# A Mamba layer on one core: the B rows broadcast to SBUF by DMA, and a fifth pair of states turned by TensorE with its products made on POOL

## The reference, cut to what matters

```python
def step(h, inp):
    xt, dt_, bt, ct = inp
    dA = jnp.exp(dt_[..., None] * A)
    h = dA * h + dt_[..., None] * bt[:, None, :] * xt[..., None]
    y = jnp.einsum('bdn,bn->bd', h, ct)
    return (h, y)
```

## Time and profile before

| what | us |
|---|---|
| three runs: median (lowest to highest) | 3478.18 (3476.75 to 3483.45) |
| the profiled execution: its own time | 3478.78 |
| its span in the trace | 3477.0 |
| phases, units in it | 64, 1024 |

### The profile page before, as it was taken

How to read it: one execution, slowest core, us unless ns; L and a number is a source line. 1 busy time by engine, 2 the same in 40 slices (tenths; PEclk the granted TensorE clock), 3 DMA queues, 4 the chain that set the end, 5 groups by cost and what they waited for, 6 DMA issues and landing times.

```text
span 3477.0 us, 53162 instructions
## 1 busy us (share of the span) xinstructions
PE 2952.8 (85%) x18432; PEld 2224.8 (64%) x18432; DVE 3042.4 (88%) x2456; ACT 3106.2 (89%) x5825; POOL 2824.1 (81%) x1701
## 2 busy tenths in 40 slices
PE   5888888888888888888888888888888888888885
PEld 3666666666666666666666666666666666666664
DVE  3889889889889888898898898899898988888986
ACT  4989999999989999999999998999999999999984
POOL 2788888888888888788788888888887888888886
PEclk9999999999999999999999999999999999999998
DMA  2222222222222222222222222222222222222221
GB/s 72 89 72 92 86 86 85 81 83 91 86 86 85 78 91 86 81 88 83 82 86 86 86 91 73 91 85 86 87 89 74 91 86 85 85 81 83 87 81 48
DMA packets 102319, 290.59 MB, mean 84 GB/s; under 512 B 11387, under 2 KB 36262, under 8 KB 102054
## 3 DMA queue, kind: packets, MB, share of 16 engines
q1 hardware_dynamic: 102054, 287.19, 25.4%
HBM read 276.91 MB, written 10.24 MB: 83 GB/s over the span
## 4 chain that ended last, share of the span: by engine, by line
ACT 33%; PE 31%; DVE 20%; issue 14%; POOL 1%; DVEq 0%; SPq 0%; DMA 0%; ACTq 0%; POOLq 0%
ACT da L697 13%; DVE hc L941 10%; PE g_ps L329 8%; DVE g_ps L928 8%; ACT w L643 7%; PE y_ps L329 5%; ACT L684 5%; PE m_ps L362 3%; PE m_ps L413 3%; PE m_ps L371 3%; PE m_ps L329 3%; PE m_ps L429 2%; PE m_ps L391 2%; DVE stats L914 2%; ACT s L667 1%
## 5 line engine op out<-in xcount | busy, mean ns | idle before, releaser
L834 POOL TENSOR_TENSOR hc<-hc,c_all 128x1000 f32<-128x1000 f32 x1024 | 2350.3, 2313 | 522.3 <-DVE hc L941 508.4
L941 DVE TENSOR_TENSOR_SCAN hc<-da,g_ps 128x1012 f32<-128x1012 f32 x1024 | 2274.6, 2253 | 91.4 <-ACT da L697 18.9
L697 ACT ACTIVATE da<-delta,a_neg 128x498 f32<-128x498 f32 x2048 | 1332.9, 700 | 9.0 <-DVE hc L941 7.3
L329 PEld LDWEIGHTS y_ps<-ident,hc 128*125 128x125 f32 x8192 | 1027.7, 190 | 238.8 <-issue 164.3
L329 PE MATMUL y_ps<-ident,hc 128*125 128x128 f32 x8192 | 1081.7, 275 | 2.2 <-POOL hc L834 2.2
L643 ACT ACTIVATE w<-ut,bt 125x256 f32<-125x256 f32 x2048 | 892.8, 497 | 2.9 <-ACT ut L630 0.4
L329 PE MATMUL g_ps<-ident,w 125*128 125x125 f32 x4096 | 547.3, 277 | 370.7 <-DVE hc L941 280.5
L329 PEld LDWEIGHTS g_ps<-ident,w 125*128 125x128 f32 x4096 | 443.9, 142 | 427.1 <-DVE hc L941 326.1
L928 DVE TENSOR_TENSOR g_ps<-u,g_ps 128x1000 f32<-128x1000 f32 x512 | 608.2, 1188 | 80.6 <-PE g_ps L455 80.3
L362 PE MATMUL m_ps<-zt,convw 128*128 128x500 f32 x1024 | 475.6, 587 | 0.7 <-ACT zt L573 0.7
L362 PEld LDWEIGHTS m_ps<-zt,convw 128*128 128x128 f32 x1024 | 190.5, 191 | 148.7 <-issue 121.9
(11 more groups left out here) (62 smaller groups left out, 2314.5 us busy)
## 6 DMA issues: line engine op xcount, KB each, us to landing
c_all<-c_rows SPq DMA_DIRECT2D x512, 500.0 KB, 3.6
xin<-x_t SPq DMA_DIRECT2D x32, 375.0 KB, 3.5
out<-out_sb SPq DMA_DIRECT2D x32, 250.0 KB
c_rows<-dbl SPq DMA_DIRECT2D x64, 31.2 KB, 1.6
c_all<-f_conv_w SPq DMA_DIRECT2D x1, 512.0 KB
c_all<-b_conv_w SPq DMA_DIRECT2D x1, 512.0 KB
hc<-f_in_w SPq DMA_DIRECT2D x1, 128.0 KB
inw<-f_in_w SPq DMA_DIRECT2D x1, 128.0 KB
```

What stands on the lines that cost most here:

```text
L329: return pe.matmul(dst, src, ident[0:rows, 0:rows], start=first, stop=last, is_transpose=True, skip_group_check=True)
L697: op = act.activation(states(da[n % RING])[j].rearrange("p (s t) -> p s t", s=SC)[:, :, 1:T], steps, ACT.Exp, scale=a_neg[:, p % 2, db, 2 ...
L834: pool.tensor_tensor(hc, hc, c_all[:, pair % CRING], ALU.mult).then_inc(hc_ready, 1)
L941: dve.tensor_tensor_scan(h[n % HRING][:, 0:UC], da[n % RING][:], g_ps[n % 2][:, 0:UC], 0.0, ALU.mult, ALU.add).then_inc(scanned, 1)
```

## The change

The straight pairs are 0, 1 and 3 now; the turned ones 2, 4, 5, 6 and 7. B's rows are written to DRAM together with C's (`write_bc`), and a DMA on SP's queue broadcasts them, two rows at a time, to the SBUF tile `b_all` (`spread_b`, 500 KB for a straight pair, two buffers, BRING). `times_b` reads `u` and `b_all`, both in SBUF, and writes `g_ps`; PE has no part in a straight unit's addend. `pick`, `split`, the bf16 parts and their copies are gone. ACT makes w for four pairs (2, 4, 5, 7), POOL for pair 6, in two instructions of 125 x 1024, each a product of `ut` and a column of `bt` that is repeated along 256 channels. `y_back` stands at units 8 and 9, `gated` at 10 and 11, and the jobs of the layer norms lie at other units.

```diff
+BRING = 2
-CONV, GATES, XPROJ, BT, SPLIT1, Y0, SPLIT2, Y1, DT, U0, U1, UT0, UT1 = 0, 4, 5, 6, 6, 6, 7, 8, 9, 11, 12, 13, 14
+CONV, GATES, XPROJ, DT, SOFTPLUS, BT, Y0, Y1, U0, U1, UT0, UT1, GATED0, GATED1 = 0, 4, 5, 6, 7, 6, 8, 9, 9, 10, 12, 13, 10, 11
-W_ACT = {2: [(-2, 4), (-1, 4)], 4: [(0, 2), (1, 2), (2, 2), (3, 2)], 6: [(6, 3), (7, 3), (8, 2)], 7: [(10, 2), (11, 3), (12, 3)]}
-W_POOL = {}
+W_ACT = {2: [(-2, 4), (-1, 4)], 4: [(0, 2), (1, 2), (2, 2), (3, 2)], 5: [(3, 1), (4, 1), (5, 2), (6, 3), (8, 1)], 7: [(10, 3), (11, 3), (12, 2)]}
+W_POOL = {6: [(6, 1), (8, 1)]}
...
-            def write_c(m):
+            def write_bc(m):
...
+            def spread_b(q):
+
+                m, v = divmod(q, len(STRAIGHT))
+                r = STRAIGHT[v]
+                sp.wait_ge(bc_written, 16 * (m + 1))
+                if q >= BRING:
+                    sp.wait_ge(dbx_ready, 2 * (q - BRING) + 2)
+                rows = bc_rows[m % 2][2 * r:2 * r + 2, :]
+                sp.dma_start(b_all[:, q % BRING], rows.partition_broadcast(128)).then_inc(b_ready[q % BRING], 16)
...
-                    pe.matmul(g[:, 0:TC], pick[:, 2 * r, :], parts[p % 2][:], start=True, stop=True)
-                    pe.matmul(g[:, BANK:UC], pick[:, 2 * r + 1, :], parts[p % 2][:],
-                              start=True, stop=True).then_inc(b_filled, 1)
...
-                op = pool.tensor_scalar(w[w_index(p, r) % WRING][:, e, j, :], ut[p % 2][:, j, :],
-                                        bt[p % 2][:, j, 2 * r + e:2 * r + e + 1], None, ALU.mult)
+                b_cols = bt[p % 2][:, :, 2 * r + n:2 * r + n + 1].broadcast_to([TP, NT, DI])
+                op = pool.tensor_tensor(w[w_index(p, r) % WRING][:, n], ut[p % 2][:], b_cols, ALU.mult)
...
-                g = paired(g_ps[n % 2])
-                dve.tensor_tensor(g, u[p % 2][:, db, :].unsqueeze(1).broadcast_to([128, 2, TC]), g,
-                                  ALU.mult).then_inc(dbx_ready, 1)
+                if n > 1:
+                    dve.wait_ge(scanned, n - 1)
+                dve.tensor_tensor(paired(g_ps[n % 2]), u[p % 2][:, db, :].unsqueeze(1).broadcast_to([128, 2, TC]),
+                                  b_all[:, q // 2 % BRING], ALU.mult).then_inc(dbx_ready, 1)
```

More of the change, by code:

```diff
@@ L86, in w_count, with straight, spread_b_step @@
     return m * len(table) + sorted(table).index(r) + 1
-def b_products(n):
+STRAIGHT = [r for r in range(PAIRS) if r not in TURNED]
+def straight(n):
     m, k = divmod(n, UNITS)
-    here = [j for j in range(k + 1) if j // 2 not in TURNED]
-    return m * 2 * (PAIRS - len(TURNED)) + len(here)
+    return m * 2 * len(STRAIGHT) + len([j for j in range(k + 1) if j // 2 in STRAIGHT])
+def spread_b_step(q):
+    m, v = divmod(q, len(STRAIGHT))
+    free = 0
+    if q >= BRING:
+        before, u = divmod(q - BRING, len(STRAIGHT))
+        free = UNITS * before + 2 * STRAIGHT[u] + 2
+    return max(UNITS * (m - 1) + XPROJ + 2, free)
@@ L96, in front_jobs, with turned_units @@
+def turned_units(n):
+    return n + 1 - straight(n)
 def front_jobs(m):
[L100 to L103, removed]
+    return [(CONV + 1, ("conv", m, 0)), (CONV + 3, ("conv", m, 1)), (GATES, ("gate", m, 0)), (GATES, ("gate", m, 1)),
+            (XPROJ, ("xproj", m, 0)), (BT, ("bt", m, 0)), (DT, ("dt", m, 0)), (DT, ("dt", m, 1))]
@@ L211, in audio_tower_kernel @@
         x_loaded = sem("x_loaded")
-        c_written = sem("c_written")
+        bc_written = sem("bc_written")
+        b_ready = [sem(f"b_ready{j}") for j in range(BRING)]
         c_ready = [sem(f"c_ready{j}") for j in range(CRING)]
@@ L303, in _ @@
                 for k in range(UNITS):
-                    if k == STORE and d == 1 and i > 0:
+                    if i > 0 and (d, k) == STORE:
                         store(i - 1)
                     if k == XPROJ + 1 and m + 1 < PHASES:
-                        write_c(m + 1)
+                        write_bc(m + 1)
+                    for q in range(straight(max(UNITS * m + k - UNITS, 0)) // 2, PHASES * len(STRAIGHT)):
+                        if spread_b_step(q) > UNITS * m + k:
+                            break
+                        if q >= BRING and spread_b_step(q) == UNITS * m + k:
+                            spread_b(q)
                     pair = (UNITS * m + k - 3) // 2 + CRING
@@ L491, in _ @@
                 i, d = divmod(m, 2)
-                front, more = m + 1 < PHASES, d == 0 and i + 1 < NCH
+                front = m + 1 < PHASES
                 for k in range(UNITS):
@@ L970, in _ @@
                     scan(n)
-                    if more and k == STATS_Z:
+                    if i + 1 < NCH and (d, k) == STATS_Z:
                         wait_drained(dve, "tokens", i + 1, 0)
```

197 lines of the change are left out of this document (85 added, 112 removed).

## The result

The changed kernel takes 3638.64 us (median of four runs, 3636.46 to 3649.92), the kernel before 3478.74 in the same comparison: 1.0465 times as long, 95% interval 1.0448 to 1.0482. The profiled execution is the longest of the four, 3649.92 us, with a span of 3647.7.

What follows compares the result with a forecast made beforehand. DVE bounded the kernel before; POOL would after: 3127 busy plus 456 of exclusion, 84.5 at its ends, 3 at the start and 64 idle gave 3735 span, 3737 us. Own range 3640 to 3880; 8-in-10 range 3310 to 3880.

Steps and rivals of the forecast that it cites:

- the exclusion: DVE's two-SBUF-input straight products and POOL's SBUF-reading instructions block each other whole; 456 us added to POOL's timeline, about 3737 us.
- The first rival: No exclusion on two-SBUF-input products: DVE needs 3065 us, POOL sets the pace, 3280 to 3345, say 3310; chance 0.20.
- the second rival: Partial interference: interleaved reads slow both, a DVE product takes twice as long, 456 us on DVE; 3440 to 3600; chance 0.08.
- POOL sets the pace: With w products and holds POOL replaces DVE as pace-setter, by a margin of 161 us, 2.5 us a phase.
- The w product: POOL's 128 new instructions of 1024 elements a partition for pair 6, taken at 2.36 us each, 303 us together.
- The holds: POOL held for the full 1.188 us of each of DVE's 384 straight products, 456 us.
- Idleness of POOL in the loop: Allowance for POOL waiting inside phase pairs, as DVE's statistics wait for POOL: 1 us a phase, 64 us.
- the partial case: Interleaved reads slowing both DVE's straight products and POOL's, about even with before: 3440 to 3600; chance 0.08.
- The tie: In runs of straight units DVE's next product and POOL's cycle both come at 3.49 us; half lost, mean wait 1.16.
- 1.2 to 2 us more: Sign expected in the changed profile: DVE's straight product, or the gap before it that POOL ends, longer by this in all.
- `gated`: Moving y_back and gated to later units removes most of DVE's 215 us of loop waits there.
- PE: Straight units' matmuls and split go, 1024 transposes come: -299 us, busy time to 2654; counts for nothing by itself.

Runs made afterwards that it cites:

- section f: Part of a test kernel of DVE and POOL instructions only: POOL reads one SBUF input beside DVE products with two; DVE's mean was 1606 ns.
- The last kernel with four pairs and B by PE: Changed kernel with B by PE, four turned pairs, no w on POOL, second dt matmul at unit 8, w between the softplus: 3471.4 us, 0.9978 of before.
- the kernel with products alone: Separate kernel computing nothing of the reference: DVE and POOL instructions side by side in eight sections, a to h; DVE products 3028 ns with both inputs in SBUF, 1198 with one in PSUM.
- the kernel with five pairs and B by PE: Changed kernel with pick and split put back, five turned pairs: 3696.42 us; with the second dt matmul moved to unit 8 and w between the softplus, 3592.36 us.
- the run with the PSUM input: Changed kernel with the straight product's second input read from PSUM, leaving out B in the straight pairs: 3361.36 us, 0.9662 of the kernel before.

## Why the prediction was right, point by point

**What bounds it, and the exclusion: shown.** The product with two SBUF inputs and POOL's products with C exclude each other. It is seen alone, it goes away with the one input, and it comes into the kernel before with it. The first rival (no exclusion, 3310) did not happen; with the exclusion taken away the kernel goes that rival's way, faster than before, though at 3361 it lies above the rival's 3280 to 3345. Of the shared slowing that the second rival assumes nothing was seen in the kernel: all 235 products of DVE that came second were held to the end of POOL's instruction. Only beside the one-input instruction of section f was the hold shorter than the instruction.

**POOL sets the pace: shown** for the changed kernel by the w instructions left out (211 us of POOL's busy time, 195 us of time) and by its idle time in the loop, which stays at 205 to 220 us.

**The sum.** Forecast for POOL: 3127 busy without holds, 456 of holds, 87.5 at the ends, 64 of other idleness, 3735 in all. In the trace: 2824.1 + 243.2 of w = 3067 without holds; 264 on the products with C (2614.5 - 2350.3) and 29 on `add_z` (70.1 - 41.0) = 293 of holds; the rest of the span, 3647.7 - 3359.3 = 288 us, is idle, some 84 of it at the ends and 204 in the loop. Three terms were mis-sized:

- The w product: 1.90 us and not 2.36, so 243 for 303. Taking the rate of a product of two full tensors for one whose second input repeats along its rows was too high.
- The holds: 293 for 456. "POOL is held for DVE's 1.188 us" should be 0.95 as measured alone and 0.89 as measured here, and not every product of DVE holds a POOL instruction: 302 products with C and 31 of `add_z` were held, against 384.
- Idleness of POOL in the loop: 204 for 64. DVE was held more often by chains that I named but priced low (108.8 us for POOL's residual), and by one that I didn't name, 87.3 us for PE's turned tiles.

Together -60 - 163 + 140 and -4 at the ends make -87: 3735 becomes 3648. The point lay 98 us above the median. The direction and the mechanism are as forecast. The size is 1 us below the forecast's own range of 3640 to 3880 and above the 3440 to 3600 of the partial case; only the wide range that covers both holds it. That the point is no farther off is partly luck: 223 us too much and 140 too little stand against each other.

**The tie.** I had DVE lose half the ties at 2.31 us each, 1.16 us in the mean; it lost 235 of 384 at 1.45 us each, 0.89 in the mean. So the sign "1.2 to 2 us more" came out too high, as did the stretched products of POOL at 3.5 us, which took 3.2. In the first units of a phase of direction 1 it is another thing: 15 products took between 6.3 and 6.5 us, while three products of POOL passed. Alone, the two engines took strict turns, so turns are not kept in every case; why they aren't there is open, and no run was made on it.

**`gated`.** "I count most of 215 us as gone from DVE" held in the wait named (11.9 us left) and not in what it is worth. The last kernel with four pairs and B by PE (3471.4) shows where it goes. DVE's groups there:

```profile
L958 DVE TENSOR_TENSOR_SCAN hc<-da,g_ps 128x1012 f32<-128x1012 f32 x1024 | 2280.2, 2253 | 144.5 <-PE g_ps L348 54.1 <-ACT da L714 20.1 <-DVE g_ps L945 1.0
L945 DVE TENSOR_TENSOR g_ps<-u,g_ps 128x1000 f32<-128x1000 f32 x512 | 608.9, 1189 | 151.9 <-PE g_ps L463 151.6
L971 DVE TENSOR_TENSOR yg<-gate,m_ps 128x500 f32<-128x500 f32 x128 | 84.9, 663 | 80.3 <-issue 51.7 <-PE m_ps L348 20.0 <-ACT delta L633 8.6
```

Against the earlier trace rows the gaps before `gated` are 142 us shorter (222.8 to 80.3), those before the straight products 71 longer (80.6 to 151.9) and those before the scans 53 longer (91.4 to 144.5). PE was late, and DVE met it elsewhere. The forecast's sum did not rest on this step, as POOL sets the pace. The first rival's 3065 us for DVE did; with the exclusion gone, 3361 was measured where it gave 3280 to 3345, and DVE waited 228.6 us for turned tiles.

**PE** was to fall to 2654 us and is at 2986. The count of matmuls is as forecast; they are longer (the transposes into `y_ps` 286 ns for 275, those into `g_ps` 297 for 277, the convolution 661 for 587), with more of them at the lower clock, which I had not looked for. **DMA**: no product waited but the first; an issue of `b_all` landed in 4.1 us.

## What to carry to other kernels

- Before an operand moves from PSUM to SBUF, count the SBUF inputs of the instruction and look at what POOL does meanwhile. A second SBUF input that costs nothing alone made the product 0.89 us longer in the mean here, and each POOL product that it held longer by as much.
- Where two engines exclude each other, add their times on one timeline and compare that sum with the span, before shifting work from one to the other: the fifth pair on POOL cost 126 us. The sum is a floor: with the same input swapped in the kernel before it gave 3517 us, and 3820 was measured.
- A stall taken from one engine's order has to be followed to the next one. Moved side jobs took 142 us of waiting from `gated`, 124 came back in front of other instructions, and the time moved by 8.

## What the runs showed of the hardware

A product of DVE with two SBUF inputs and a POOL product of two SBUF inputs don't overlap: the second is held until the first is done, and its own record is longer (DVE up to 3.29 us for 1.20, POOL 3.24 for 2.29), with no idle gap shown. In the changed kernel a held DVE product ends 1.06 us after POOL's instruction, 0.12 less than its free length, so it is let go shortly before that instruction's recorded end. With one DVE input in PSUM, or a POOL instruction that only writes, neither is held.

POOL's product of two inputs runs at 2.29 us for 1000 elements on 128 partitions, and at 1.90 us for 1024 on 125 when one input repeats an element 256 times; with one tensor and a constant, section f of the kernel with products alone, an instruction that met no product of DVE took 2.71 us for 1000, longer than with two tensors.

PE's lower clock took 135 us before, 668 in the changed kernel, and 491 with zero matmuls in its straight units. Idle straight units don't explain it: the kernel with five pairs and B by PE fills them and has 654 us, and the run with the PSUM input leaves them idle and has 436. What brings the low stretches stays open; one of them, shown above, began as PE resumed after an idle time of 2.75 us.
